# The last group of layer 1's self-attention: who makes the weighted values, where the projections land, when the residuals run

## What is computed

```python
def _L1_attn_ref(src, in_proj_weight, in_proj_bias, out_proj_weight, out_proj_bias):
    s, b, f = src.shape            # 4 tokens, 512 positions, 256 features
    h, d = (16, 64)
    qkv = jnp.einsum('sbf,pf->sbp', src, in_proj_weight) + in_proj_bias
    q, k, v = jnp.split(qkv, 3, axis=-1)
    ...
    attn = jax.nn.softmax(jnp.einsum('nsd,ntd->nst', q / 8, k), axis=-1)
    out = jnp.einsum('nst,ntd->nsd', attn, v)      # o[s] = sum over t of attn[s, t] * v[t]
    out = out @ out_proj_weight.T + out_proj_bias
x = _layernorm(x + _L1_attn_ref(x, ...), axis=-1)
```

## Time and profile before

| | us |
|---|---|
| median of 3 runs | 2319.09 |
| lowest and highest of them | 2316.57, 2324.06 |
| the profiled execution, device time | 2316.37 |
| its span, first to last instruction | 2314.6 |
| layer 1's self-attention, all of it | about 616 to 909 of the span |
| from the last chunk that PE fills to the last normed row | 866 to 909 of the span |

### The profile page before, as it was taken

One profiled execution on the slowest core, in us unless ns is written; L12 is line 12 of the kernel. 1 busy time (PEld: TensorE's weight loads), 2 busy tenths in 40 slices (PEclk: granted clock), 3 DMA queues, 4 the chain that ended last, 5 costly groups with the idle time before them and its releaser, 6 DMA issues. The chain is left out here.

```text
span 2314.6 us, 35756 instructions
## 1 busy us (share of the span) xinstructions
PE 2003.6 (87%) x12692; PEld 1393.6 (60%) x12692; DVE 1533.4 (66%) x2470; ACT 1153.9 (50%) x2213; POOL 953.6 (41%) x749
## 2 busy tenths in 40 slices
PE   7888858994988983889999999999999996799992
PEld 4565537992343443556666666565666664699992
DVE  5687864553978795588788768887787886222224
ACT  3332311102357544568776777677776772233332
POOL 2233222322222131066675756675566665222223
PEclk9999978997999996899999999999999998799996
DMA  4100017211000001000000000000000001621113
GB/s 154 39 30 14 25 69 277 102 33 59 1 0 1 0 1 65 29 1 1 29 1 1 10 6 25 1 10 1 1 1 1 10 1 65 236 83 38 38 33 118
DMA packets 36715, 93.30 MB, mean 40 GB/s; under 512 B 5415, under 2 KB 24379, under 8 KB 31934
## 3 DMA queue, kind: packets, MB, share of 16 engines
q1 hardware_dynamic: 30462, 74.72, 9.0%
q0 software_dynamic: 6080, 16.29, 2.1%
HBM read 76.56 MB, written 14.44 MB: 39 GB/s over the span
## 5 line engine op out<-in xcount | busy, mean ns | idle before, releaser
L1984 POOL TENSOR_TENSOR x_total<-x_total,x_pt 128x1024 f32<-128x1024 f32 x189 | 446.7, 2364 | 175.5 <-ACT x_pt L2070 158.0
L2091 ACT ACTIVATE x_pt<-PS,x_maskf 128x512 f32<-128x512 f32 x544 | 332.5, 689 | 168.0 <-PE PS L2394 166.0
L2190 DVE TENSOR_TENSOR PS<-x_pt,PS 128x512 f32<-128x512 f32 x480 | 333.4, 695 | 65.9 <-ACT x_pt L2091 28.6
L2208 DVE TENSOR_TENSOR x_pt<-x_pt,PS 128x1024 f32<-128x1024 f32 x320 | 320.3, 1052 | 0.7 <-PE PS L2412 0.7
L2394 PE MATMUL PS<-x_qs,x_ks 64*128 64x256 f32 x2176 | 281.9, 395 | 1.5 <-ACT x_pt L2091 1.5
L2371 PE MATMUL PS<-x_pt,x_vs 128*64 128x256 f32 x2108 | 262.9, 388 | 20.2 <-ACT x_pt L2070 10.7
L2070 ACT ACTIVATE x_pt<-x_pt 128x1536 f32<-128x1536 f32 (+1 forms) x160 | 266.5, 1667 | 12.3 <-DVE x_pt L2208 12.1
L1143 PEld LDWEIGHTS PS<-m_xT,m_own 128*128 128x128 f32 x1984 | 235.0, 195 | 7.0 <-DVE m_own L1219 2.9
L2394 PEld LDWEIGHTS PS<-x_qs,x_ks 64*128 64x128 f32 x2176 | 199.2, 188 | 65.1 <-issue 39.1
L1143 PE MATMUL PS<-m_xT,m_own 128*128 128x128 f32 x1984 | 235.9, 278 | 2.8 <-DVE m_own L1219 2.4
L2371 PEld LDWEIGHTS PS<-x_pt,x_vs 128*64 128x64 f32 x2108 | 141.9, 137 | 137.5 <-issue 63.8
(11 more groups left out here) (294 smaller groups left out, 2830.3 us busy)
## 6 DMA issues: line engine op xcount, KB each, us to landing
f_w<-in_L_ffn_w SPq DMA_DIRECT2D x32, 1024.0 KB
a_ctxT<-in_ctxT SPq DMA_DIRECT2D x8, 800.5 KB, 4.3
f_w<-ys SPq DMA_DIRECT2D x24, 256.0 KB, 5.2
x_cx<-in_ctx SPq DMA_DIRECT2D x4, 1536.0 KB
l_w<-in_L_attn_w SPq DMA_DIRECT2D x6, 512.0 KB
a_xT<-in_xT SPq DMA_DIRECT2D x4, 512.0 KB, 5.2
X<-in_x SPq DMA_DIRECT2D x1, 2048.0 KB, 11.2
xr<-a_xn SPq DMA_DIRECT2D x16, 128.0 KB, 1.7
```

Of the source, the lines that this page charges most:

```text
L1984: ins = nc.gpsimd.tensor_tensor(total2[:], first, tile[:, 2 * k + 2:2 * k + 4, :], ALU.add)
L2091: nc.scalar.activation(pt[:, s % 2, t, :].rearrange("p (h n) -> p h n", h=2), PS[:, first:first + 2, half], ACT.Identity, bias=maskf[:, b ...
L2190: ins = nc.vector.tensor_tensor(acc, tile, acc, ALU.max)
L2208: nc.vector.tensor_tensor(p_, p_, PS[:, MB, None, :].to_broadcast([P, at.stop - at.start, SPAN]), ALU.subtract).then_inc(lowered, 1)
```

## The change

Only the last group is changed; groups 0 to 2 issue what they issued before.

- **Weighted values.** ACT weighs t = 2 for all four tokens, and t = 3 for token 0 alone: five of (s, t) where there were six (`weigh_last`). `wp` alternates by its number k. DVE makes the value of t = 3 for tokens 1, 2 and 3 (L1663 of the new file), adds it (L1664), and then adds ACT's (L1666), token by token.
- **ACT's order** is (0,2), (0,3), (1,2), copy o[0], (2,2), copy o[1], (3,2), copy o[2], copy o[3].
- **Projections** of the last group go to banks 0 and 1 of the ring, which is idle by then. They wait for the ring to be free, and no longer for the residuals of group 2. `residual` reads them there.
- **Residuals** of group 2 stand behind the sums of group 3 on DVE.

```diff
+            def weigh_last(s, t, k):
+                last = J - 1
...
+                act.wait_ge(ring_free, last * USES + QK + 2 * t + 2)
+                if k < 2:
+                    act.wait_ge(third_added if k == 0 else o_ready, last * B)
+                elif k == 2:
+                    act.wait_ge(third_added, last * B + 1)
+                else:
+                    act.wait_ge(o_ready, last * B + k - 2)
+                for h in range(H1):
+                    ins = nc.scalar.activation(wp[:, k % 2, h * HD1:(h + 1) * HD1],
+                                               qkv[:, last % 2, t, 2 * P1 + h * HD1:2 * P1 + (h + 1) * HD1],
+                                               ACT.Copy, scale=sc[:, last % 2, s, t, h:h + 1])
+                ins.then_inc(wp_ready, 1)
...
             def residual(grp, s):
+                bank = PB + s // 2 if grp < J - 1 else s // 2
...
-                if grp == J - 1:
-                    add(grp, 0, 2)
-                    add(grp, 0, 3)
-                if grp >= 1:
+                if 1 <= grp < J - 1:
                     for s in range(B):
                         residual(grp - 1, s)
-            last, s = J - 1, B - 1
-            add(last, 1, 2)
-            add(last, 1, 3)
+            last = J - 1
+            add(last, 0, 2)
+            add(last, 0, 3)
             dve.wait_ge(own_ready, J * B)
             dve.wait_ge(ring_free, J * USES)
-            for t in (2, 3):
-                link(nc.vector.tensor_tensor(by_head(prod[:, t % 2, :]), heads(last, t, 2), share(last, s, t), ALU.mult))
-            link(nc.vector.tensor_tensor(o[:, s, :], o[:, s, :], prod[:, 0, :], ALU.add))
-            add(last, 2, 2)
-            add(last, 2, 3)
-            nc.vector.tensor_tensor(o[:, s, :], o[:, s, :], prod[:, 1, :], ALU.add).then_inc(o_ready, 1)
+            for s in range(1, B):
+                link(nc.vector.tensor_tensor(by_head(prod[:, s % 2, :]), heads(last, 3, 2), share(last, s, 3), ALU.mult))
+                link(nc.vector.tensor_tensor(o[:, s, :], o[:, s, :], prod[:, s % 2, :], ALU.add))
+                dve.wait_ge(wp_ready, 2 * last * B + 2 + s)
+                nc.vector.tensor_tensor(o[:, s, :], o[:, s, :], wp[:, (s + 1) % 2, :], ALU.add).then_inc(o_ready, 1)
+            for s in range(B):
+                residual(last - 1, s)
             norm(last - 1, 0)
             norm(last - 1, 1)
...
-                if grp >= 1:
+                if grp == J - 1:
+                    pe.wait_ge(ring_free, J * USES)
+                elif grp >= 1:
                     pe.wait_ge(r_ready, grp * B)
-                out = PS[:, PB + s // 2, (s % 2) * D:(s % 2 + 1) * D]
+                bank = PB + s // 2 if grp < J - 1 else s // 2
+                out = PS[:, bank, (s % 2) * D:(s % 2 + 1) * D]
```

More of the change, by code:

```diff
@@ L1531, in _ @@
                     made = weigh_to(grp, made, min(made + (0 if u < 2 else 3 if u < 6 else 2), 16 if u < 6 else 24 if u < 10 else 32))
[L1532 to L1537, removed]
+            def weigh_last(s, t, k):
+                last = J - 1
+                if s == 0 and t == 2:
+                    act.wait_ge(attn_ready, last + 1)
+                act.wait_ge(ring_free, last * USES + QK + 2 * t + 2)
[10 more added lines that the diff above has]
+                ins.then_inc(wp_ready, 1)
+            weigh_last(0, 2, 0)
+            weigh_last(0, 3, 1)
+            weigh_last(1, 2, 2)
+            turned(J - 1, 0)
+            weigh_last(2, 2, 3)
+            turned(J - 1, 1)
+            weigh_last(3, 2, 4)
+            turned(J - 1, 2)
+            turned(J - 1, 3)
         @block.vector
@@ L1554, in residual @@
                     dve.wait_ge(x_ready, grp * B)
-                nc.vector.tensor_tensor(r[:, s, :], PS[:, PB + s // 2, (s % 2) * D:(s % 2 + 1) * D], tile(s, grp), ALU.add)\
+                nc.vector.tensor_tensor(r[:, s, :], PS[:, bank, (s % 2) * D:(s % 2 + 1) * D], tile(s, grp), ALU.add)\
                     .then_inc(r_ready, 1)
```

## The result

The changed kernel takes 2304.81 us (median of 4 runs, 2303.82 to 2307.13), the kernel before in the same comparison 2318.53. The ratio is 0.9945, with a 95% interval of 0.9929 to 0.9961: 12.7 us faster by the ratio (13.7 between the two medians), where 5.3 were forecast. The two intervals overlap, and both stand clear of the forecast's 0.9977.

The account below looks back on a forecast made before the run. Bound by the self-attention block's end: ACT and DVE until o[1], then mostly PE. PE's chain from 879.42, 18.42 plus 2.2 us low clock, ends 5.3 us earlier: 2319.09 - 5.3 = 2313.8 us, range 2308.8 to 2319.0.

Parts of the forecast that it names:

- the chain: Last group's PE work from turn 1 to the last project: unbroken, ending 5.3 us earlier; chance 0.57.
- turn 1: PE's transposing of token 1's sum in the last group: starts at 879.42 instead of 883.26 us.
- The two waits of DVE for ACT: At tokens 2 and 3 of the last group, DVE waits about a microsecond each for ACT's weighted value.
- The end of PE's work: PE's last project in the last group ends at 900.04 us, not 905.36.
- The block's end: Last norm of the self-attention block: unchanged 4.08 us after the last projection, ending near 904.1 us.
- the mask's wait: Next block's first DVE step waits for a transfer issued behind the barrier; stays 8.15 us.
- the term for the clock: In the last group's PE chain, low clock until 883.8 us costs 2.2 us, between 1.9 and 2.5.
- an earlier end moves the whole rest forward by as much: Behind the block: the next starts from a barrier, so the full 5.3 us reach the span.
- as many can be won as lost: Argument against low-clock stretches behind the block adding 3.3 to 3.9 us of gain; that rival had chance 0.21.
- more than the chain: Rival: low-clock stretches behind the block fall otherwise, giving 3.3 to 3.9 us more, near 2310.3 us; chance 0.21.
- The count from turn 1's first transpose: In the last group, the clock's rise is counted from turn 1's start at 879.42: 4.4 us, to 883.8.
- The 0.04 in the prediction's list: Rival: the last group's chain gains less because the clock rises later; chance 0.04.

Follow-up runs that it names:

- e2_ring: Kernel before with only the last group's projections moved to ring banks, waiting for the ring and not the residuals; ratio 0.9997.
- e3_resid: Kernel before with last-group projections in ring banks and group 2's residuals behind the sums, old sharing of weighted values; ratio 0.9993.
- e4_share: Changed kernel's sharing of weighted values alone: projection banks as before, group 2's residuals ahead of token 1's sums; ratio 0.9961 to the kernel before.
- w4_unbroken: Changed kernel with TensorE's idle stretches filled by 76, 24 and 156 unread identity transposes, pauses included; ratio 0.9953 to the kernel before.
- e8_late: Kernel before with one unread full-width VectorE add more behind the last norm; ratio 0.9973, median 2308.38 us against 2315.42.
- e7_delay3: Changed kernel with three full-width VectorE adds more at the end of its block; 2313.06 us, ratio 0.9991 to the kernel before.
- e1_delay: Changed kernel with four full-width and one half-width VectorE add more at its block's end; median 2314.17 us, ratio 0.9992 to the kernel before.
- w2_next: Changed kernel with 136 unread identity transposes on TensorE at the start of the next block; ratio 0.9962 to the kernel before.
- e5_delay1: Changed kernel with one full-width VectorE add more at its block's end; ratio 0.9959 to the kernel before, runs in clusters at 2299.8–2300.8 and 2309.5–2311.4 us.
- w1_attn: Changed kernel with 64 unread identity transposes on TensorE between its last chunk and turn 0; ratio 0.9964 to the kernel before.
- e10_late_again: The kernel of e8_late, timed a second time against the kernel before; ratio 0.9989, median 2312.97 us against 2317.43.
- a1_again: The changed kernel with nothing edited, timed a second time against the kernel before; ratio 0.9958.

## Why the prediction was wrong

**Right, and to about 0.3 us:** the chain. Counted from the first sum, turn 1 was put at 6.96 us and came at 7.06. The two waits of DVE for ACT were put at about a microsecond each and were 1.11. The end of PE's work was put at 27.58 and came at 27.28; the low clock from turn 1 on lasted 4.2 us, not 4.4. The block's end was put 5.3 us earlier and came 5.62. PE had no gap, the residuals of group 2 didn't hold the last ones (a wait of 2.73 us was left, put at 3), and the mask's wait stayed at 8.0. e2_ring, e3_resid and e4_share confirm the pieces. w4_unbroken confirms the term for the clock, at 1.91 us where the sum had 2.2.

**Wrong:** the step "an earlier end moves the whole rest forward by as much", which stood in the first part and carried the sum to the span. The rest is not rigid. It has low-clock stretches whose number and place hang on when it starts (20.5 to 39.5 us in sum over the 17 profiles). The argument with which I had put the rival aside, "as many can be won as lost", takes the place for random. It isn't: in all 14 profiles in which TensorE was idle there, the work stands in the same place against the clock's changes at this point. The clock fell 2.46 us before the first sum in the profile before, 2.42 before it after, and 2.33 to 2.43 in the twelve others, although the first sum itself lay anywhere from 870.7 to 878.9. The windows around it in the profile before, and after:

```profile
869.00:870.00 1.00, 0.00 (x0) 1.00 0.00 0
```

```profile
870.00:871.00 1.00, 0.00 (x0) 0.86 0.00 0
871.00:872.00 1.00, 0.00 (x0) 0.50 0.00 0
```

With the earlier trace rows the first says that before the clock fell at 870.0; the second that it fell within 870 to 871 after, where the first sum is at 873.13. Why the program meets the clock's changes alike each time no run shows. That the place counts is shown by e8_late and its repeat, where a delay alone made the kernel before faster, and by e4_share; each shift but e4_share's also put an instruction more into VectorE's stream, and no run separates the two. So the shift of 5.6 us was not thrown anew in each run: both profiles of the changed kernel follow one new pattern for 730 us behind the first sum, and have less low clock than the kernel before (27.9 and 21.2 us for 35.8).

**Mis-sized with it:** the rival "more than the chain" was the right mechanism, with 3.3 to 3.9 us and a chance of 0.21. The first result has 7 us of surplus and the second 4. The range's lower end, 2308.8, was built from that price and missed 2304.81. The kernel before sat in a bad place: it has 35.8 us of low clock, and e2_ring and e3_resid, which end their block at the same place, 39.5 and 39.4. Of the profiles whose block ends elsewhere only e7_delay3's (34.3 us) comes near; the others have 20.5 to 30.1. But e1_delay, put back to the old place, has 28.9, so the place is a large part of it and not all.

**The count from turn 1's first transpose:** the rows bear it out. In w4_unbroken the clock stayed at 1.00 through 76 transposes, turn 0, 24 more and turn 1, and in w2_next it rose 3.2 us into a row of nothing but transposes (from 905.36; the windows have 0.51 from 905.4 to 908.6 and 1.00 from there). In the changed kernel it rose at 884.4, 4.2 us after turn 1's first transpose at 880.19, between the 3.8 and the 5.0 us that the prediction had read from the trace before. So to count from that transpose was right. The 0.04 in the prediction's list stood for a chain that gains less because the clock rises later. No run shows that term: both profiles of the changed kernel have the block 5.6 us shorter (31.36 and 31.35 us, before 36.98).

**Open:** why e7_delay3 and e4_share part at 0.2 us of difference, and e1_delay and the kernel before at 0.05; which of the stretches decides between the two clusters of e5_delay1; and how large the surplus is (4 us by one comparison, 7 by the other).

## What to carry to other kernels

When an edit shortens a block, the block's own gain can be worked out from unit costs to a few tenths (5.3 us against a measured 5.62 here), but the total isn't less by just that (12.7 and 9.7 us here). The kernels here, whose profiles show 20.5 to 39.5 us of low clock behind the block, answered to a shift, a pure delay included, by several us more or less than the shift's own length: in the kernel before one add of 1.27 us behind the last norm gave 0.9973 and 0.9989, some 6 and 3 us less time instead of 1.3 more. So judge an edit by marks inside the profile, from the same instruction to the same instruction, and before crediting the total to the edit, time the old kernel with a delay as well. Where two engines each hold a step for nearly the same time, as the residuals and the fourth weighted value did here, moving either alone can leave that step where it was: turn 1 came 10.80 us after the first sum in e3_resid and 10.79 in e4_share, as in the kernel before, and 7.06 after it only with both.

## What the runs showed of the hardware

- One full-width VectorE add more on the critical path made the kernel before faster, 0.9973 [0.9957, 0.9989] and 0.9989 [0.9977, 1.0001] in two comparisons, and two and a half such adds made it slower, 1.0010 [1.0001, 1.0020].
- Transposes of a resident 128x128 tile ran at 0.113 us each at the high clock (7.21 us for 64), and kept it there (w4_unbroken, 1.00 from 866 to 899). In w1_attn the high clock was lost 2.9 us after the filling's end, behind a pause of 1.7 us, 1.1 us of transposes and 0.1 us of the next pause.
- Low-clock stretches came back at the same distances from the first sum in two profiles of one kernel, to 0.1 us: all six up to 1930 us in e8_late and e10_late_again, the first five in the changed kernel and a1_again.
- Over 17 profiles a microsecond of low clock in the cross block cost 0.45 us of span.
